# Three score buffers in the first attention, and another order of steps in the delta stage

## The reference

```python
Q = (X @ Wq.T + bq).reshape(B, S, H, d_head) * scale
K = (X @ Wk.T + bk).reshape(B, S, H, d_head) * scale
V = (X @ Wv.T + bv).reshape(B, S, H, d_head)
scores = jnp.einsum('bqhd,bkhd->bhqk', Q, K)
scores = jnp.where(causal[None, None], scores, -jnp.inf)
attn = jax.nn.softmax(scores.astype(jnp.float32), axis=-1).astype(X.dtype)
out = jnp.einsum('bhqk,bkhd->bqhd', attn, V).reshape(B, S, D)
```

```python
qkv = jax.nn.silu(_causal_conv1d(qkv, conv_weight))
attn = -(jnp.einsum('bhcid,bhcjd->bhcij', k_beta, k) * decay_mask)
attn, _ = jax.lax.scan(_correct_row, attn, jnp.arange(1, chunk_size))
v_prime = v_c - jnp.einsum('bhld,bhde->bhle', kcd_c, state)
out = inter + jnp.einsum('bhij,bhjd->bhid', intra, v_prime)
new_state = state * gel_c[..., None] + jnp.einsum('bhld,bhle->bhde', k_c * kd_c, v_prime)
```

## Time and profile before

| | |
|---|---|
| median of 3 runs | 1867.23 us (1865.87 to 1867.99) |
| profiled execution | 1864.84 us, its span 1863.1 us |
| PE busy | 1552.3 us, 83% |
| DVE busy | 1205.6 us, 65% |
| ACT busy | 861.8 us, 46% |
| POOL busy | 738.2 us, 40% |
| score maxima | about 43 to 168 us |
| steady part of the delta stage | 725 to 1507 us, 12 periods of 63.2 to 69.2 us |

### The profile page before, as it was taken

How to read it: one execution, slowest core, us unless ns; L and a number is a source line. 1 busy time by engine, 2 the same in 40 slices (tenths; PEclk the granted TensorE clock), 3 DMA queues, 4 the chain that set the end, 5 groups by cost and what they waited for, 6 DMA issues and landing times. The chain is left out here.

```text
span 1863.1 us, 39066 instructions
## 1 busy us (share of the span) xinstructions
PE 1552.3 (83%) x14453; PEld 1069.3 (57%) x14453; DVE 1205.6 (65%) x2406; ACT 861.8 (46%) x2356; POOL 738.2 (40%) x1048
## 2 busy tenths in 40 slices
PE   5877983297444899999999999999999999749998
PEld 2443342264322666766776677677667767635554
DVE  6776127732555778778778887877888786333443
ACT  2223851142133666666656656665665664311111
POOL 6000000375114356656645665564566565400000
PEclk9998996598767999999999999998999999869999
DMA  7000004085522556465545646464564654110111
GB/s 231 1 2 2 2 1 141 24 268 169 158 60 54 120 138 166 102 158 138 150 113 136 166 109 158 130 152 109 138 166 102 160 135 113 52 40 28 39 38 44
DMA packets 226773, 196.38 MB, mean 105 GB/s; under 512 B 87202, under 2 KB 203810, under 8 KB 224544
## 3 DMA queue, kind: packets, MB, share of 16 engines
q1 hardware_dynamic: 218720, 180.35, 36.8%
q0 software_dynamic: 3456, 9.43, 1.6%
q10 hardware_dynamic: 4416, 4.20, 0.7%
HBM read 121.79 MB, written 72.03 MB: 104 GB/s over the span
## 5 line engine op out<-in xcount | busy, mean ns | idle before, releaser
L1600 PE MATMUL d_big<-all_xn_t,all_w 128*128 128x512 f32 x512 | 262.2, 638 | 45.8 <-DVE d_conv L1818 39.2
L1818 DVE SCALAR_TENSOR_TENSOR d_conv<-d_big,all_cw,d_conv 128x1023 f32<-128x1023 f32 (+2 forms) x192 | 245.6, 1279 | 70.2 <-ACT d_conv L1982 66.2
L1600 PEld LDWEIGHTS d_big<-all_xn_t,all_w 128*128 128x128 f32 x512 | 93.2, 199 | 124.0 <-issue 83.1
L2168 POOL TENSOR_TENSOR d_y<-d_y,all_xn 128x256 f32<-128x256 f32 x128 | 105.2, 822 | 126.1 <-DVE d_y L1961 66.8
L1789 PE MATMUL d_big<-all_wo,d_yt 128*128 128x256 f32 x512 | 127.6, 395 | 12.5 <-DVE d_yt L1888 12.5
L2082 ACT COPY d_ys<-d_big 128x128 f32<-128x128 f32 x256 | 62.5, 267 | 157.7 <-PE d_big L1751 137.8
L2374 PE MATMUL e_gu<-all_xn_t,all_last_up 128*128 128x512 f32 x272 | 122.2, 603 | 12.6 <-DVEq L2402 12.6
L1722 PE MATMUL d_big<-all_w,all_xn_t 128*128 128x256 f32 x512 | 126.0, 390 | 0.1
L2125 POOL TENSOR_TENSOR d_vs<-d_vs,d_sv 128x1024 f32<-128x1024 f32 x32 | 61.3, 1915 | 152.6 <-DMA d_vs<-turned_v_scratch 151.4
L1862 DVE SCALAR_TENSOR_TENSOR d_AI<-d_big,d_b_col,d_decay 128x256 f32<-128x256 f32 x256 | 104.6, 476 | 20.6 <-PE d_big L1613 19.8
L324 DVE TENSOR_REDUCE a_neg_max<-a_big 128x1 f32<-128x128 f32 (+7 forms) x128 | 90.0, 752 | 32.3 <-PE a_big L257 31.9
(11 more groups left out here) (359 smaller groups left out, 3733.3 us busy)
## 6 DMA issues: line engine op xcount, KB each, us to landing
turned_kq_scratch<-d_turned SPq DMA_DIRECT2D x32, 512.0 KB, 4.0
d_kq_tok<-turned_kq_scratch SPq DMA_DIRECT2D x128, 128.0 KB, 3.4
turned_v_scratch<-d_vs SPq DMA_DIRECT2D x16, 1024.0 KB, 5.0
d_vs<-turned_v_scratch SPq DMA_DIRECT2D x64, 256.0 KB, 6.5
grouped_y_scratch<-d_yx SPq DMA_DIRECT2D x32, 512.0 KB, 3.0
d_yx<-grouped_y_scratch SPq DMA_DIRECT2D x128, 128.0 KB, 3.6
all_w<-in_L_attn_W_qkvz SPq DMA_DIRECT2D x16, 768.0 KB
l_hold<-in_L_ffn_gate_up_proj SPq DMA_DIRECT2D x48, 192.0 KB, 3.4
```

Of the source, the lines that this page charges most:

```text
L1600: mm = pe.matmul(big[0][:, c, :], w_sb[par][:, k, n * DK:(n + 1) * DK], xn_t[:, k, c * 512:(c + 1) * 512], start=(k == 0), stop=(k == KD - 1))
L1818: dve.scalar_tensor_tensor(conv[:, sh:T], src[:, 0:T - sh], cw[:, bass.ds(g, 1), COLUMN_OF[j], 3 - sh], conv[:, sh:T], ALU.mult, ALU.add). ...
L2168: pool.tensor_tensor(part, part, zs[:, t, :], ALU.mult).then_inc(s["yg_s"], 1)
```

## The change

Attention: the score tiles go round three buffers, `big[2]`, `big[3]` and `big[1]`, and `scores` waits for the reduction three tiles back. The turns, the values and the transposed maxima share the two banks of `big[0]` in alternation. A turn is cut into four quarters of three matmuls and 512 columns, which stand behind tiles 1, 2, 3 and 4, and ScalarE casts each quarter on its own. Before a bank is used again, TensorE waits for the reader of the step two before in the list `side`.

Delta stage: the five tables are new. No step is added or taken away. The diff, cut to its core:

```diff
+        NBUF = 3
+        score_buf = [big[2], big[3], big[1]]
+        side = [("turn", 0, quarter) for quarter in range(4)]
+        for h in range(H0):
+            side += [("turn", h + 1, quarter) for quarter in range(4 if h + 1 < H0 else 0)]
+            side += [("values", h)] if h < TT else []
+            side += [("maxima", 0)] if h == HALF else []
...
+            def free(k):
...
+                kind, *at = side[k - 2]
+                if kind == "turn":
+                    pe.wait_ge(rows_s, 4 * at[0] + at[1] + 1)
+                elif kind == "values":
+                    pe.wait_ge(v_out, at[0] + 1)
+                else:
+                    pe.wait_ge(maxp, 4 * at[0] + 4)
...
-                if i >= 2:
-                    pe.wait_ge(s_max, i - 1)
+                if i >= NBUF:
+                    pe.wait_ge(s_max, i - NBUF + 1)
...
-                buf = big[2 + q % 2]
+                buf = score_buf[i % NBUF]
...
-                    if h + 1 < H0 and q in (2, 5):
-                        turn(h + 1, q // 3)
+                    if h + 1 < H0 and 1 <= q <= 4:
+                        turn(h + 1, q - 1)
...
-                    act.copy(rows[0:MAXROW, h, :], big[n][0:MAXROW, :, :].rearrange("p c n -> p (c n)")).then_inc(rows_s, 1)
+                    act.copy((q_rows, k_rows)[n][0:MAXROW, h, c * 512:(c + 1) * 512],
+                             bank[side_at["turn", h, quarter] % 2][0:MAXROW, :]).then_inc(rows_s, 1)
...
-    prev y_out 0; next kq_out 0; this v_out; prev y_in 0; next kq_in 0; this v_in; next kq_out 1, kq_in 1; prev y_out 1;
-    next blocks; prev y_in 1; this weights; next rows, solved; prev wo
+    this solved, v_out; prev y_out 0; next kq_out 0; prev y_in 0; this v_in; next kq_in 0; this weights; next kq_out 1,
+    rows; prev y_out 1; next blocks; prev y_in 1; next kq_in 1; prev wo
```

More of the change, by code:

```diff
@@ L191, in attention0_phase @@
         unit_ps = [big[2], big[3], big[0], big[1]]
+        NBUF = 3
[5 more added lines that the diff above has]
+            side += [("maxima", 0)] if h == HALF else []
+        side += [("maxima", 1)]
+        side_at = {step: k for k, step in enumerate(side)}
         @block.sync
@@ L1329 @@
-    kv 5; prev out_mm 1 0; this ks 6, iv 5, qs 6, y 6; prev out_mm 1 1; this kv 6
+    next proj 0 0; prev ks 7; next proj 0 1; prev qs 7, iv 6; this gates 0; prev y 7; this gates 1, l0p 0, l0p 1, l0p 2,
+    l0p 3, l0p 4; next proj 1 0, proj 1 1; this l0p 5, l0p 6, l0p 7; prev iv 7; this gates 2, l0y 0, l0y 1, l0y 2, l0y
+    3, l0y 4, l0y 5, l0y 6, l0y 7; next proj 2 0, proj 2 1; this l1p 0, l1p 1, l1p 2, l1p 3, gates 3; next products 0;
+    this l1y 0, l1y 1, l1y 2, l1y 3; next products 1; this l2p 0; next proj 3 0, proj 3 1; this l2p 1, l2y 0; next
@@ L1335 @@
-    this l1y; next tap 2 3, kb; this l2p; next products 0, products 1; this l2y; next products 2, products 3; this state
-    0, r 1, gather 0, state 1, r 2, gather 1, state 2, gather 2, r 3; next tap 3 1; prev out_mm 0 0; this state 3, r 4,
-    gather 3, state 4, r 5; prev y_turn 1; this state 5, gather 4; prev out_mm 0 1; this r 6; next tap 3 2, tap 3 3,
-    v_turn 0; this state 6; prev out_mm 1 0, out_mm 1 1
+    prev state 6; this v_turn 0; prev gather 5, r 7; this v_turn 1; next tap 0 1, tap 0 2, tap 0 3, shift, kq_turn 0;
@@ new lines @@
+    prev gather 6; this qe, l0p; next tap 1 1, tap 1 2, tap 1 3; prev gather 7, y_turn 0; this l0x; next kq_turn 1; this
+    l1p; next tap 2 1, tap 2 2, tap 2 3; this l1y; next kb; this l2p; next products 0, products 1; this l2y; next
+    products 2, products 3; this state 0, r 1, gather 0; prev out_mm 0 0; this state 1, r 2, gather 1, state 2, gather
+    2, r 3; next tap 3 1; prev out_mm 0 1; this state 3, r 4, gather 3, state 4, r 5; prev y_turn 1; this state 5,
+    gather 4; next tap 3 2; this r 6; prev out_mm 1 0; next tap 3 3; prev out_mm 1 1
@@ L1339 @@
 """)
 ACT_ORDER = steps_of("""
-    next tap0 0; this gates 0; prev ys 7, sq2 4, o1 7; next silu 0, decay, tap0 1; this gates 1, gates 2, l0y; next silu
-    1, ksq 0, tap0 2; this l1p; next ksq 1; this gates 3; next ksq 2, ksq 3; prev sq2 5; this l1y, l2p; prev sq2 6, sq2
-    7; this l2y, ys 0; next qsq 0, silu 2; this ys 1, o1 1, ys 2, o1 2; next tap0 3; this sq2 0, ys 3, o1 3, ys 4, o1 4,
-    sq2 1, ys 5, o1 5, sq2 2; next qsq 1; this o1 6, ys 6; next silu 3; this sq2 3
+    prev sq2 2, sq2 3; this silu 3; next tap0 0; prev sq2 4, ys 7; this qsq 1; next silu 0; this gates 0; prev sq2 5;
@@ L1346 @@
+    next tap0 1; this gates 1; prev sq2 6; this gates 2; prev o1 7; next silu 1; this l0y; next ksq 0, tap0 2, ksq 1;
+    this gates 3, l1p; next ksq 2, ksq 3, decay; this l1y; prev sq2 7; this l2p; next silu 2; this l2y, ys 0, ys 1, o1
+    1, ys 2, o1 2; next tap0 3; this ys 3, o1 3, ys 4, sq2 0, o1 4, ys 5, o1 5, sq2 1; next qsq 0; this ys 6, o1 6
 """)
 POOL_ORDER = steps_of("""
-    next gdiff; prev yn 0, gate 5; this kout; next cross; this kb; prev gate 6, gate 7; this vs 0; prev wo; this vs 1;
@@ L1350 @@
-    prev norm 1, yn 1; this gate 0, gate 1, gate 2; next solve 0, solve 1, solve 2, solve 3, solve 4; this gate 3, norm
-    0, gate 4
+    prev norm 0, yn 0; next gdiff; prev gate 5; this kout; prev gate 6, wo; next cross; this kb, vs 0; prev gate 7; this
+    vs 1; prev norm 1, yn 1; this gate 0, gate 1, gate 2; next solve 0, solve 1, solve 2, solve 3, solve 4; this gate 3,
+    gate 4
 """)
```

73 lines of the change are left out of this document (35 added, 38 removed).

## The result

The changed kernel took 1930.83 us (median of 4 runs, 1927.92 to 1939.63) against 1866.55 (1863.51 to 1867.99) for the kernel before: a ratio of 1.036, interval [1.0337, 1.0384]. The profiled execution took 1927.92 us, its span 1926.1. The prediction, 1846 (1826 to 1868), has the wrong sign. The attention stage did what it says and gained 16 us; the delta stage lost 79, about five times as much.

What follows compares the result with a forecast made beforehand. Bound: VectorE and TensorE waiting for each other in attention (too few buffers), a nearly dense TensorE in the delta stage. 1864.8 - 16 (attention) - 4 (12 delta periods) = 1844.8, about 1847 against the median; forecast 1846 us, range 1826 to 1868.

Steps and rivals of the forecast that it cites:

- Rival D: Attention stage: it gains only half of the 16 us, through a quarter-cast chain or lower clock; 1855 us, chance 0.18.
- First move: Delta stage: v_turn 1 and v_out go ahead of the taps; third projection waits 0.8 instead of 1.35 us, alone gaining nothing.
- K: Delta stage: start of `ksq 0` on ScalarE, the first square of the transposed keys, once they have landed.
- Second move: Delta stage, SyncE's order: v_out leaves from ahead of kq_in 0, v_in comes there; K 1.2 us earlier per period.
- Both ends that it drew for K: Bounds on the start of `ksq 0`: 3.4 us earlier with engines to itself, 0.3 earlier if v_in must be through first.
- second bound: Delta stage: v_in must be through before kq_in 0, issued by about 924.5, landing 6.5 later; K only 0.3 us earlier.
- The count of bytes: Delta stage: 2.5 MB with kq_in 0 as before, at 208 GB/s 12.0 us, since v_in replaces v_out ahead of it.
- Rival C: Delta stage: K 0.9 us late, 0.9 more behind it, clock falling every period; 1884 us, chance 0.14.
- Third move: Delta stage: ksq 1 and gates 3 go before l1p on ScalarE; l1y at K + 4.1, y 0 at K + 16.3, 0.9 us lost.
- `solved` behind `wo`: Delta stage: costed at nothing; if the cover by TensorE's other work is short, l0p waits up to 0.5 us per period.

## Why the prediction was wrong

**Attention: right.** Predicted waits of 0.3, 0.3 and 0.2 in a head were 0.43, 0.29 and 0.21; the head of 6.5 to 6.9 us was 6.85; the stage ends 16 us earlier, and VectorE's waits fell to the 15 us forecast. No cast appears among TensorE's waits. Term by term: heads 1 to 8 gave 0.91 us each (0.9 was said), the later heads 1.04 to 1.1 (1.0 was said). The two terms taken without a count were both off and nearly cancel, which is luck: head 9 gave 0.8 instead of 2, head 0 gave 1.9 instead of 1. Following one buffer chain with durations of rows was enough for the rest. Rival D fell.

**First move: half right.** The third projection's wait fell from 14.7 us in twelve periods to 9.3, which is the 0.8 us a period that was said. But the text saw no gain in the move itself, and let v_in eat up what v_out gave. In the old order, with v_in left behind the keys, it is worth 24 us, through K.

**Second move, K: the step that failed.** The text took K 1.2 us earlier, and it came 1.2 later (13.20 to 14.43). Both ends that it drew for K were earlier than before, so no loss was inside the K term. The term that was wrong is v_in's issuing in the second bound, "issued by about 924.5", which is 4.3 us after kq_out 0. SyncE starts v_in's four issues only behind y_in's, at 3.8, and ends them at 6.0 on average (at 7.0 in the period shown, 933.02 - 926.04). The rest of that bound held: v_in landed 6.7 us after its last issue (6.5 was taken) and the keys 1.8 behind it (2.5 was taken). With 6.0 in place of 4.3 the bound gives K at 15.0 us after kq_out 0, against 13.2 before and 14.4 measured. The count of bytes ("2.5 MB with kq_in 0 as before") did not see this either: it leaves out that kq_in 0 is issued behind v_in's issues, and that 1 MB just ahead of the keys costs 4.3 us where v_out, with y_in 0 between it and them, had cost 3.1. Rival C had the later K, and its 0.9 us was the nearest. A smaller slip: the base of 13.55 us was one period, and the mean of the twelve is 13.20.

The Trainium skill, "DMA: Bandwidth & Descriptors", section "Two DMAs through the same engine are not ordered", was cited for descriptors that start in order, by which K would gain 0.3 us only. The trace agrees with it (issued behind v_in, the keys land 1.8 us behind it). The gain of 0.3 that was drawn from it came out wrong through the issue time of v_in.

**Third move, behind K: right at full clock.** l1y at K + 4.1 was 4.09; y 0 at K + 16.3 was 16.39 in the one period whose clock stayed full. But the forecast counted with that clock and with a wait of 1 to 2 us. The wait was 3.60 us on average, and the clock fell in eleven of twelve periods: more falls than before stood in the sum at nothing, and they cost 28 us (next paragraph).

**Rival C had the mechanism and less than half of the price,** 33 us for the delta stage where it lost 79. Its condition (keys held behind v_in's issues, TensorE's wait at l1y above 2.5 us, the clock falling every period) is what happened, but for one period. It said 2 us of delay per period, and the rows give 2.0: 1.2 ahead of K, and 0.8 behind it (16.39 against 15.62, the mean of before's six periods at full clock). It mis-sized the clock: 1.5 us more in half the periods, from one pair of windows in the earlier trace rows, where the clock in K to y 0 had only fallen to 0.90. After fell to 0.74 to 0.82 there, and that stretch is 3.6 us longer than at full clock (20.0 against 16.4). Over the twelve periods the clock cost 40 us behind K (12 times 19.71 - 16.39) where it had cost 12 (12 times 16.65 - 15.62): 28 more instead of 9. And it priced no group outside the steady twelve, which gave 21 us more. From y 0 to kq_out 0 the orders were called nearly alike; they differ by 0.5 us a period, 6 us. Some 0.2 of it is VectorE's `shift`, which takes 1.7 us instead of 1.5 in eleven of the twelve periods; why, and where the rest lies, is left open. Together 24 + 28 + 6 + 21 - 16 = 63, the difference of the spans.

**`solved` behind `wo`**: TensorE waited for it four times, 3.2 us in all. Small, as said.

**What the chain shows.** The prediction asked of each moved DMA what it passes, and not which engine's step now depends on its early landing. In the changed order v_in *had* to be early, because vs 0 had come ahead of gate 7 on GpSimd. Undoing the visible fault alone made the kernel slower (1943), and undoing both made it faster than before (1839).

## What to carry to other kernels

When a load moves ahead of another on the same queue, charge the one behind with the first one's issuing time, counted from where SyncE really gets to it, and with its bytes, and let the upper bound be a later landing; equal megabytes elsewhere in the row do not cancel it. Then follow, on every engine, the first step that waits for a moved transfer and what is queued behind it: the orders of the engines hang together, and one step put back alone can be worse than none. And where the bound engine is dense, price a wait of some 3 us not at 3 but with the slower clock behind it, here about as much again (3.3 us behind a wait of 3.6).
